# A four-layer graph network on one core: the last pass over nodes moved into the second GCN stage, with narrower PSUM slots

## The chip, the cores and the metric

The kernel runs on one core of a Trainium2 chip. The metric is the device time of one execution in microseconds; lower is better. All data are fp32. TensorE (PE in the profile, PEld for its weight loads), VectorE (DVE), ScalarE (ACT), GpSimd (POOL) and SyncE (SP) run side by side and wait for each other through semaphores. A DMA is issued from the queue of ScalarE, SyncE or GpSimd.

## What is computed

A graph of 100,000 nodes with 64 features and 50,000 edges, sorted by destination, goes through four layers. Each adds its result to x after a layer norm and a relu. The change touches the last one, a GCN of two convolutions, 64 to 32 features and back to 64:

```
def gcn_conv(x, src, dst, W, b):
    deg = segment_sum(ones_like(src), dst, n)
    dinv = where(deg > 0, rsqrt(deg), 0.0)
    norm = dinv[src] * dinv[dst]
    h = x @ W
    return segment_sum(h[src] * norm[:, None], dst, n) + b

src, dst = add_self_loops(edge_index, n)
h = relu(layernorm(x))
x = x + gcn_conv(relu(gcn_conv(h, src, dst, W1, b1)), src, dst, W2, b2)
```

The destinations are drawn as 100,000 u² with u uniform in 0 to 1: low nodes have many edges, high ones few.

## The kernel before

Nodes lie in 784 tiles of 128 (one node per partition), edges in 392 tiles of 128. Since destinations are sorted, edges and node tiles are walked together as a staircase of 74 blocks of `S` = 16 steps. A step adds one edge tile to one node tile and moves on either to the next edge tile or to the next node tile. Which it is depends on the data, so the steps of a block are loaded into registers from the small tables `g.steps` and `g.blocks` in SBUF, which `setup` makes.

The GCN consists of three stages at the end of the program, each with a block of code for every engine. An earlier stage (`sk` in the trace) has made the table t3, x @ W1 scaled by dinv, and stored x as `g.x3`.

`gcn_edges` runs twice, as first stage (t3 to t4) and as second stage (t4 to the tensor `gcn_acc` in SBUF). GpSimd gathers 128 message rows of 32 values per instruction, in 49 batches of 8 (L897 is the gather's helper line); SyncE counts the batches that arrived (L2039). VectorE makes the one-hots of a block, `hot`, in one comparison (L2095). TensorE opens the PSUM `ring` by products with the all-zero `blank` (L2071, and L2079 in mid-ring), and then adds 16 products of a one-hot with a piece of `msgs` (L2080), each to the slot of its node tile. Every fp32 product shows as two records in the trace. A slot is 128 columns wide, four times the 32 that are needed; the message columns are repeated to fill it. Two blocks are in flight: one uses the banks 0 to 3, the other 6 to 3, so they share bank 3, and its blank has to wait for the add of the block before. VectorE adds the 16 slots to the window of `gcn_acc` (L2106). In the first stage it then closes 16 tiles per block in three operations (L2121 to L2123) and ScalarE stores them; in the second stage nothing follows.

`gcn_close` is the third stage (`gf` in the trace): 49 steps of 16 tiles. VectorE scales `gcn_acc` by dinv (L2154), TensorE transposes four pieces (helper L733), ScalarE copies them to SBUF (L2179), TensorE multiplies with W2 (helper L741, N = 256), GpSimd adds the bias to the loaded x (L2203), VectorE adds the product to x (L2161), and ScalarE stores to `out` (L2191). Loads go over SyncE's queue (L2146), up to six steps ahead, stores over ScalarE's.

## Time and profile before

| | us |
|---|---|
| median of 3 runs | 6699.57 (6690.15 to 6706.76) |
| the profiled execution | 6710.78 |
| its span on the core | 6709.1 |
| busy PE / PEld | 4395.3 / 3843.5 |
| busy DVE / ACT / POOL | 4366.9 / 1838.5 / 3785.6 |

Busy shares of the whole span mix many stages. Of the 6709.1 us the three GCN stages are the last 1,268; how each is limited has to be read from its own stretch. In a timeline a row is one instruction or several merged ones ("x24"), with its start, its length, and in brackets how long its engine was idle before and what ended that. The length of a merged row reaches to the end of its last member.

### The profile page before, as it was taken

Reading aid. Unit: us, or ns where it says so; the run is one execution under the profiler, and the core shown is the slowest. Engines: PE = TensorE matmul, PEld = TensorE weight load, DVE = VectorE, ACT = ScalarE, POOL = GpSimd, SP = SyncE. Lnnn points to the kernel's source line nnn. Section 1 sums busy time; section 2 is a strip of 40 time slices with the busy share of each in tenths; the row PEclk is TensorE's granted clock in tenths of the full one; section 3 lists DMA queues with packets and bytes.
Section 4 is the critical chain, followed back from the end, with each engine's and each line's share of the span. In section 5 each row is a group of like instructions: output and inputs, shape, how many; then the busy total and the mean of one; then the engine's idle time right before and its main releaser. Section 6 shows DMA issues by size and latency. Waiting matters only on the chain. (4 is left out here: it accounts for less than half of the span.)

```text
span 6709.1 us, 96894 instructions
## 1 busy us (share of the span) xinstructions
PE 4395.3 (66%) x29117; PEld 3843.5 (57%) x29194; DVE 4366.9 (65%) x5674; ACT 1838.5 (27%) x2782; POOL 3785.6 (56%) x3348
## 2 busy tenths in 40 slices
PE   6665445771078878566565877766787856865887
PEld 3454344661067777555555865555787745755775
DVE  7898544224667778778798852224988955862458
ACT  5543112330033444333333421111453410000001
POOL 0398665773077757577763767774000047757756
PEclk9766667996589999877778988889998978988999
DMA  6398766677955558433334864544678851231109
GB/s 239 93 276 264 160 143 145 142 142 257 394 174 167 174 177 260 149 99 95 98 105 135 272 185 139 144 138 131 211 254 298 309 192 42 58 123 14 14 17 300
DMA packets 865593, 1128.43 MB, mean 168 GB/s; under 512 B 591583, under 2 KB 604276, under 8 KB 864060
## 3 DMA queue, kind: packets, MB, share of 16 engines
q1 hardware_dynamic: 409660, 807.13, 35.8%
q10 hardware_dynamic: 311296, 226.11, 11.1%
q0 software_dynamic: 144256, 90.12, 9.3%
q8 instruction: 239, 3.92, 0.2%
q14 instruction: 142, 1.16, 0.1%
HBM read 633.88 MB, written 495.44 MB: 168 GB/s over the span
## 5 line engine op out<-in xcount | busy, mean ns | idle before, releaser
L897 POOL DMA_INDIRECT gc_msgs<-t,src_rows x784 | 753.6, 961 | 1112.9 <-POOLq L148 816.2
L2080 PE MATMUL gc_ring<-gc_msgs,gc_hot 128*128 x4736 | 650.9, 296 | 239.0 <-SPq L2039 233.7
L2080 PEld LDWEIGHTS gc_ring<-gc_msgs,gc_hot 128*128 128x128 f32 x4736 | 624.2, 209 | 310.5 <-issue 303.1
L951 POOL DMA_INDIRECT acc<-de_sums,de_put x392 | 607.6, 1550 | 303.8 <-issue 149.8
L897 POOL DMA_INDIRECT edge_rows<-h,dst_rows x392 | 379.7, 969 | 231.7 <-issue 116.5
L897 POOL DMA_INDIRECT at1s_ends<-x,src_rows x392 | 409.8, 1045 | 168.7 <-issue 117.4
L897 POOL DMA_INDIRECT edge_rows<-x,dst_rows x392 | 387.7, 989 | 166.4 <-issue 117.4
L897 POOL DMA_INDIRECT re_rows<-x,src_rows x392 | 405.9, 1035 | 125.4 <-issue 125.1
L897 POOL DMA_INDIRECT at2s_ends<-h,src_rows x392 | 370.8, 946 | 142.4 <-issue 119.0
L1503 PE MATMUL re_psR<-w_rel,re_own 128*128 128x128 f32 x3136 | 396.2, 292 | 71.7 <-DVE re_own L1440 71.3
L1503 PEld LDWEIGHTS re_psR<-w_rel,re_own 128*128 128x128 f32 x3136 | 388.9, 207 | 80.5 <-issue 77.8
L2106 DVE TENSOR_TENSOR gcn_acc<-gcn_acc,gc_ring 128x512 f32 x148 | 101.7, 687 | 427.8 <-PE gc_ring L2080 427.8
L2095 DVE TENSOR_TENSOR gc_hot<-gc_fixed,steep 128x2048 f32<-128x2048 f32 x148 | 338.0, 2284 | 64.4 <-DMA gcn_acc<-t 64.4
L2179 ACT ACTIVATE gf_uT<-gf_psT 128x512 f32<-128x512 f32 x49 | 29.3, 597 | 1237.7 <-PE gf_psT L733 1237.7
L1033 DVE TENSOR_TENSOR de_sums<-de_sums,de_ring 128x64 f32 x74 | 16.4, 221 | 519.1 <-PE de_ring L1076 519.1
L1764 DVE TENSOR_TENSOR at2s_outs<-at2s_psY,at2s_own_b 128x512 f32<-128x512 f32 x196 | 135.6, 692 | 320.4 <-PE at2s_psY L741 314.1
L1076 PE MATMUL de_ring<-de_win,de_pick 128*128 x2368 | 336.3, 302 | 0.1
L1056 PE MATMUL de_ps_pick<-de_near,de_hot 128*128 x1184 | 152.8, 245 | 275.2 <-issue 233.7
L1076 PEld LDWEIGHTS de_ring<-de_win,de_pick 128*128 128x128 f32 x2368 | 321.6, 216 | 16.9 <-issue 11.0
L1301 PE MATMUL rew_ring<-rew_local,rew_hot 128*128 (+1 forms) x2368 | 283.2, 278 | 71.7 <-issue 40.4
L1301 PE MATMUL at1w_ring<-at1w_local,at1w_hot 128*128 (+1 forms) x2368 | 284.8, 279 | 62.8 <-issue 46.7
L1301 PE MATMUL at2w_ring<-at2w_local,at2w_hot 128*128 (+1 forms) x2368 | 283.5, 278 | 57.6 <-issue 45.2
(539 smaller groups left out, 11250.2 us busy)
## 6 DMA issues: line engine op xcount, KB each, us to landing
rew_win<-x SPq DMA_DIRECT2D x74, 544.0 KB
at1w_win<-g SPq DMA_DIRECT2D x74, 544.0 KB
at2w_win<-g SPq DMA_DIRECT2D x74, 544.0 KB, 4.1
de_win<-t ACTq DMA_DIRECT2D x74, 512.0 KB, 4.5
de_near<-same SPq DMA_DIRECT2D x74, 512.0 KB, 5.0
x<-rew_win SPq DMA_DIRECT2D x74, 512.0 KB
h<-at1w_win SPq DMA_DIRECT2D x74, 512.0 KB
h<-at2w_win SPq DMA_DIRECT2D x74, 512.0 KB, 2.9
```

The costliest lines, as they stand in the source:

```text
L897: nc.gpsimd.indirect_dma_start(buf[:, t * width:(t + 1) * width], None, table, bass.IndirectOffsetOnAxis(ap=rows[:, t:t + 1], axis=0)).the ...
L951: nc.gpsimd.indirect_dma_start(g.acc0[j % LANES], bass.IndirectOffsetOnAxis(ap=put[:, j:j + 1], axis=0), sums[:, j * D:(j + 1) * D], None, ...
L1033: v.tensor_tensor(here, here, low[n % 2][:, 0:D], ALU.add).then_inc(joined, 1)
L1056: done = nc.tensor.matmul(ps_pick[u % 2][:, n * P:(n + 1) * P], hot[m % 2][:, h * HALF + n, :], near[m % 3][:, bass.ds(of[n], P)], start=T ...
L1076: done = nc.tensor.matmul(ring[:, bass.ds(both[n], 2 * D)], pick[u % 2][:, n, :], win[k][:, bass.ds(both[HALF + n], 2 * D)], start=False, ...
L1301: done = nc.tensor.matmul(to[:, bass.ds(at[n], SLOT)], hot[k][:, n, :], of[:, bass.ds(at[n], SLOT)], start=False, stop=(n == S - 1), skip_ ...
L1503: last = nc.tensor.matmul(psR[s][:, t * P:(t + 1) * P], own[q][:, t * P:(t + 1) * P], each_group(g.w["rel"][:, q * D:(q + 1) * D], 2), sta ...
L1764: nc.vector.tensor_tensor(to, psY[:, :].rearrange("p (q n w) -> p q n w", n=N2, w=P), own_b[:, :, :, :].rearrange("p n u d -> p n (u d)"). ...
L2080: done = nc.tensor.matmul(ring[:, bass.ds(to[n], SLOT)], hot[k][:, n, :], each_group(msgs[:, bass.ds(of[n], MID)], SLOT // MID), start=Fal ...
L2095: nc.vector.tensor_tensor(hot[m % 2][:, :, :], each_group(fixed[:, 0:P], S), spread(g.steep[:, m * S:(m + 1) * S], P), ALU.is_equal).then_ ...
L2106: nc.vector.tensor_tensor(grouped(window, MID), grouped(window, MID), slots[(m - 1) % 2][:, :, 0:MID], ALU.add).then_inc(added, 1)
L2179: nc.scalar.activation(uT[b.slot % 2][:, :], psT[b.slot % 2][:, :], ACT.Copy).then_inc(evac, 1)
```

## The change

`gcn_close` is removed. Its work is done within the second call of `gcn_edges`, which now gets `out`: after each block's add, VectorE scales the 16 tiles that no later block changes (`scaled`), TensorE transposes them (`tip`), ScalarE copies the result (`turn`) and writes the broadcast bias into the PSUM `psO` (`fill`), TensorE accumulates the product with W2 onto it (`project`), VectorE adds `psO` to the loaded x (`finish`, three blocks later), and ScalarE stores. ScalarE issues both the loads and the stores. The groups follow the blocks, so there are 74 of 16 tiles instead of 49; neighbouring groups overlap and some tiles are written more than once with ever later sums. A store waits for the one before to land. There are two `scaled` and `scaledT`, four `x`, one `psT` and one `psO`. Where each group lies is held in four new columns of `g.blocks`, made in `setup`.

In both calls a PSUM slot is 64 columns wide instead of 128. The ring of one block takes two banks, the two blocks in flight share none, two blanks open it, and nothing is waited for in mid-ring.

```diff
@@ build
-        g.blocks = keep("blocks", [P, 6], i32)
+        g.blocks = keep("blocks", [P, 10], i32)
...
-            gcn_edges(nc, g, "gc1", g.t3, acc, g.t4)
-            gcn_edges(nc, g, "gc2", g.t4, acc, None)
-            gcn_close(nc, g, acc, out)
+            gcn_edges(nc, g, "gc1", g.t3, acc, g.t4, None)
+            gcn_edges(nc, g, "gc2", g.t4, acc, None, out)
@@ setup
+                link(v.tensor_scalar(turn[:, :], ended[:, :], float(WHOLE - S), None, ALU.min))
+                for n, unit in enumerate((1, MID, D, P)):
+                    v.tensor_scalar(g.blocks[:, 6 + n:7 + n], turn[:, :], float(unit), None, ALU.mult)
@@ gcn_edges, tiles
-        ring, fixed = r.ps("ring", [P, RING]), r.ps("fixed", [P, 512])
+        ring, fixed = r.ps("ring", [P, NARROW_RING]), r.ps("fixed", [P, 512])
+        half = NARROW_RING // 2
+            scaled, scaledT = ([r.sb(f"{n}{k}", [P, S * MID]) for k in range(2)] for n in ("scaled", "scaledT"))
+            x = [r.sb(f"x{k}", [P, S * D]) for k in range(4)]
+            psT, psO = r.ps("psT", [P, S * MID]), r.ps("psO", [P, S * D])
@@ gcn_edges, ScalarE of the second stage
+                    def load(m):
...
+                        if m > 4:
+                            act.wait_ge(done_out, 16 * (m - 4))
+                        act.dma_start(x[m % 4][:, :], part).then_inc(x_in[m % 4], 16)
+                    def turn(m):
+                        act.wait_ge(tipped, m)
...
+                        nc.scalar.activation(scaledT[m % 2][:, :], psT[:, :], ACT.Copy).then_inc(tip_copied, 1)
+                    def fill(m):
+                        if m > 1:
+                            act.wait_ge(ready, m - 1)
+                        nc.scalar.activation(grouped(psO[:, :], D), each_group(g.w["bg2"][:, :], S), ACT.Copy).then_inc(filled, 1)
+                    def store(m):
+                        act.wait_ge(ready, m)
+                        if m > 1:
+                            act.wait_ge(done_out, 16 * (m - 1))
+                        if m < BLOCKS:
+                            first = place(nc.scalar, m, 9, (WHOLE - S) * P)
+                            act.dma_start(out[bass.ds(first, S * P), :].rearrange("(j p) d -> p j d", p=P), grouped(x[m % 4][:, :], D)).then_inc(done_out, 16)
...
+                    load(1)
+                    load(2)
+                    for m in range(1, BLOCKS + 1):
+                        turn(m)
+                        fill(m)
+                        if m > 1:
+                            store(m - 1)
+                        if m + 2 <= BLOCKS:
+                            load(m + 2)
+                    store(BLOCKS)
@@ gcn_edges, TensorE
+                def tip(m):
+                    pe.wait_ge(scaled_made, m)
+                    if m > 1:
+                        pe.wait_ge(tip_copied, m - 1)
+                    transpose_pairs(nc, psT, scaled[m % 2], g.ident, S // 4).then_inc(tipped, 1)
+                def project(m):
+                    pe.wait_ge(tip_copied, m)
+                    pe.wait_ge(filled, m)
+                    times(nc, psO, scaledT[m % 2], g.w["gcn2"], S // 4, start=False).then_inc(projected, 1)
...
-                    for h in banks[k][0:3]:
-                        nc.tensor.matmul(ring[:, h * 512:(h + 1) * 512], blank[:, 0:P], blank[:, :], start=True, stop=False, skip_group_check=True)
+                        for h in range(k * half, (k + 1) * half, 512):
+                            nc.tensor.matmul(ring[:, h:h + 512], blank[:, 0:P], blank[:, :], start=True, stop=False, skip_group_check=True)
...
-                        if n == LAST_BANK:
-                            if m >= 1:
-                                pe.wait_ge(added, m)
-                            h = banks[k][3]
-                            nc.tensor.matmul(ring[:, h * 512:(h + 1) * 512], blank[:, 0:P], blank[:, :], start=True, stop=False, skip_group_check=True)
-                        done = nc.tensor.matmul(ring[:, bass.ds(to[n], SLOT)], hot[k][:, n, :],
-                                                each_group(msgs[:, bass.ds(of[n], MID)], SLOT // MID),
-                                                start=False, stop=(n == S - 1), skip_group_check=True)
+                            last = nc.tensor.matmul(ring[:, bass.ds(to[n], NARROW)], hot[k][:, n, :],
+                                                    each_group(msgs[:, bass.ds(of[n], MID)], NARROW // MID),
+                                                    start=False, stop=(n == S - 1), skip_group_check=True)
...
+                    if out is not None:
+                        if 1 <= m - 1 <= BLOCKS:
+                            tip(m - 1)
+                        if 1 <= m - 2 <= BLOCKS:
+                            project(m - 2)
@@ gcn_edges, VectorE
+                def finish(m):
+                    dve.wait_ge(x_in[m % 4], 16 * ((m - 1) // 4 + 1) if m % 4 else 16 * (m // 4))
+                    dve.wait_ge(projected, m)
+                    nc.vector.tensor_tensor(x[m % 4][:, :], x[m % 4][:, :], psO[:, :], ALU.add).then_inc(ready, 1)
...
+                    if m >= 1 and middle is None:
...
+                        dve.wait_ge(added, m)
+                        if m > 2:
+                            dve.wait_ge(tipped, m - 2)
+                        nc.vector.tensor_tensor(grouped(scaled[m % 2][:, :], MID), grouped(ended, MID), dinv, ALU.mult).then_inc(scaled_made, 1)
+                        if m > 3:
+                            finish(m - 3)
```

What stands in a row on TensorE where one block of the second stage ends and the next begins, before (an ISA row at L2080 or L2148 is the address step of the product behind it, a TENSOR_LOAD reads registers from SBUF):

```order
L2080 MATMUL gc_ring<-gc_msgs,gc_hot 128x128
L2064 TENSOR_LOAD steps
L2071 MATMUL gc_ring<-gc_blank 128x512 x3
L2072 TENSOR_LOAD blocks
L2072 ISA x2
L2080 ISA
L2080 MATMUL gc_ring<-gc_msgs,gc_hot 128x128
```

TensorE at the same place of the second stage now:

```order
L2148 MATMUL gc_ring<-gc_msgs,gc_hot 128x64
L738 MATMUL gc_psT<-ident,gc_scaled 128x128 x4
L746 MATMUL gc_psO<-w_gcn,gc_scaledT 128x256 x4
L2137 TENSOR_LOAD steps
L2144 MATMUL gc_ring<-gc_blank 128x512 x2
L2145 TENSOR_LOAD blocks
L2145 ISA x2
L2148 ISA
L2148 MATMUL gc_ring<-gc_msgs,gc_hot 128x64
```

Four transposes and four products (of 256 columns) have come between the last product of a ring and the register load of the next block, and two blanks of three are left at the start.

On ScalarE, one step in the middle of the last pass before:

```order
L2194 ISA
L2178 REGISTER_ALU
L2179 ACTIVATE gf_uT<-gf_psT 128x512
L2191 ISA
L2191 DMA out_x<-gf_x 128x16x64
```

ScalarE over one block in the middle of the second stage now, where it had nothing before:

```order
L2089 ACTIVATE gc_scaledT<-gc_psT 128x512
L2094 ACTIVATE gc_psO<-b_bg 128x1024
L2056 TENSOR_LOAD blocks
L2102 ISA
L2102 DMA out_x<-gc_x 128x16x64
L2056 TENSOR_LOAD blocks
L2083 REGISTER_ALU
L2083 DMA gc_x<-x 128x1024
```

A second activation, the load of x and two register loads have joined the copy and the store.

On VectorE, one block of the second stage before:

```order
L2095 TENSOR_TENSOR gc_hot<-gc_fixed,steep 128x2048
L2101 TENSOR_LOAD blocks
L2106 ISA
L2106 TENSOR_TENSOR gcn_acc<-gcn_acc,gc_ring 128x512
L2095 TENSOR_TENSOR gc_hot<-gc_fixed,steep 128x2048
```

VectorE over one block of the second stage now:

```order
L2174 TENSOR_TENSOR gc_hot<-gc_fixed,steep 128x2048
L2056 TENSOR_LOAD blocks
L2185 ISA
L2185 TENSOR_TENSOR gcn_acc<-gcn_acc,gc_ring 128x512
L2206 TENSOR_LOAD blocks
L2216 ISA
L2216 TENSOR_TENSOR gc_scaled<-gcn_acc,dinv 128x512
L2168 TENSOR_TENSOR gc_x<-gc_x,gc_psO 128x1024
L2174 TENSOR_TENSOR gc_hot<-gc_fixed,steep 128x2048
```

The scaling and the last add, of a group three blocks older, have moved between the add of a block and the one-hots of the next but one.

## Rows read from the trace of the kernel before

**Rows 1.** Windows: stretch, us, busy PE, PEld, DVE, ACT, POOL; granted clock, DMA share, GB/s.
```profile
5441.00:6001.00 560.00, 384.48 (x2626) 329.40 (x2664) 367.19 (x373) 0.00 (x0) 382.87 (x392) 0.88 0.24 71
6001.00:6537.00 536.00, 385.22 (x2627) 330.66 (x2664) 214.77 (x152) 0.00 (x0) 370.73 (x392) 0.88 0.15 37
6537.00:6709.10 172.10, 127.64 (x588) 95.27 (x588) 141.64 (x98) 29.26 (x49) 116.91 (x49) 0.96 1.07 298
```

**Rows 2.** Waits of the second stage (who waited for whom: us, times, longest).
```profile
...
PE gc_ring L2080 <- SPq L2039: 118.0, 20, 31.0
...
```

**Rows 3.** Timeline, second stage, GpSimd: start us, us, engine line op [idle before].
```profile
6249.63 0.95 POOL L897 DMA_INDIRECT gc_msgs<-t,src_rows  x1 [0.31 <-issue]
```

**Rows 4.** Timeline, second stage, VectorE: adds of blocks 12, 21, 30, 35 and 74.
```profile
6167.42 0.69 DVE L2106 TENSOR_TENSOR gcn_acc<-gcn_acc,gc_ring 128x512 f32 x1 [4.27 <-PE gc_ring L2080]
...
6239.26 0.69 DVE L2106 TENSOR_TENSOR gcn_acc<-gcn_acc,gc_ring 128x512 f32 x1 [7.14 <-PE gc_ring L2080]
...
6300.30 0.69 DVE L2106 TENSOR_TENSOR gcn_acc<-gcn_acc,gc_ring 128x512 f32 x1 [9.22 <-PE gc_ring L2080]
...
6329.03 0.69 DVE L2106 TENSOR_TENSOR gcn_acc<-gcn_acc,gc_ring 128x512 f32 x1 [6.02 <-PE gc_ring L2080]
...
6535.21 0.69 DVE L2106 TENSOR_TENSOR gcn_acc<-gcn_acc,gc_ring 128x512 f32 x1 [4.57 <-PE gc_ring L2080]
```

**Rows 5.** Timeline, second stage, weight loads: one late block.
```profile
6387.01 0.34 PEld L2071 LDWEIGHTS gc_ring<-gc_blank 128*128 128x128 bf16 x3 [0.59 <-issue]
6387.81 2.75 PEld L2080 LDWEIGHTS gc_ring<-gc_msgs,gc_hot 128*128 128x128 f32 x24 [0.46 <-issue]
6390.49 0.10 PEld L2079 LDWEIGHTS gc_ring<-gc_blank 128*128 128x128 bf16 x1
...
6392.23 0.34 PEld L2071 LDWEIGHTS gc_ring<-gc_blank 128*128 128x128 bf16 x3 [0.56 <-issue]
```

**Rows 6.** Timeline, second stage, weight loads after a ring at a lower clock.
```profile
6237.85 1.08 PEld L2080 LDWEIGHTS gc_ring<-gc_msgs,gc_hot 128*128 128x128 f32 x8
6238.85 0.42 PEld L2071 LDWEIGHTS gc_ring<-gc_blank 128*128 128x128 bf16 x3
```

**Rows 7.** Timeline, stage before the GCN, TensorE: products 64 and 128 columns wide.
```profile
5296.04 2.00 PE L741 MATMUL sk_psO<-w_gcn,sk_hT 128*128 128x64 f32 x16 [1.82 <-ACT sk_hT L1951]
5297.87 2.00 PE L741 MATMUL sk_psB<-w_skip_b,sk_g2T 128*128 128x128 f32 x16
```

**Rows 8.** Timeline, last pass, TensorE: the products, then the transposes of one tile.
```profile
6644.81 1.99 PE L741 MATMUL gf_psH<-w_gcn,gf_uT 128*128 128x256 f32 x8 [0.69 <-ACT gf_uT L2179]
6646.64 0.60 PE L733 MATMUL gf_psT<-ident,gf_u 128*128 128x128 f32 x4
```

**Rows 9.** Timeline, first stage, weight loads: a late block opens.
```profile
5859.49 0.34 PEld L2071 LDWEIGHTS gc_ring<-gc_blank 128*128 128x128 bf16 x3 [1.12 <-issue]
```

**Rows 10.** Timeline, first stage, VectorE: adds of blocks 35 and 74, one block between.
```profile
5774.68 0.69 DVE L2106 TENSOR_TENSOR gcn_acc<-gcn_acc,gc_ring 128x512 f32 x1 [5.66 <-PE gc_ring L2080]
...
5858.71 0.69 DVE L2106 TENSOR_TENSOR gcn_acc<-gcn_acc,gc_ring 128x512 f32 x1 [0.41 <-PE gc_ring L2080]
...
5861.61 2.28 DVE L2095 TENSOR_TENSOR gc_hot<-gc_fixed,steep 128x2048 f32<-128x2048 f32 x1
...
5995.21 0.69 DVE L2106 TENSOR_TENSOR gcn_acc<-gcn_acc,gc_ring 128x512 f32 x1 [2.57 <-PE gc_ring L2080]
```

**Rows 11.** Instructions of three tiles: ns min/median/max, first and last start us.
```profile
L2154 DVE TENSOR_TENSOR gf_u<-gcn_acc,dinv x49: 685/1905/2480, 6536.9 to 6696.8; 128x512 f32 x42, 128x512 f32<-128x512 f32 x7
...
L2161 DVE TENSOR_TENSOR gf_x<-gf_x,gf_psH x49: 1207/1222/1223, 6543.6 to 6702.3; 128x1024 f32<-128x1024 f32 x49
...
L1266 ACT ACTIVATE rew_ring<-rew_blank x74: 807/810/1437, 2403.0 to 2741.3; 128x780 f32<-128x780 f32 x72, 128x1536 f32<-128x1536 f32 x2
```

**Rows 12.** Tile out_x in the last pass: issue to landing of its stores.
```profile
DMA to landing us min/median/max: 3.8/6.1/7.0
```

**Rows 13.** Timeline, last pass, VectorE: its last add.
```profile
6702.27 1.22 DVE L2161 TENSOR_TENSOR gf_x<-gf_x,gf_psH 128x1024 f32<-128x1024 f32 x1 [2.24 <-PE gf_psH L741]
```

More of the change, by code:

```diff
@@ L2003, in _, with gcn_edges @@
                 pipeline(dve, order=[(3, close), (2, variance), (1, add)], slots=DEEP)
-def gcn_edges(nc, g, name, nodes, acc, middle):
+def gcn_edges(nc, g, name, nodes, acc, middle, out):
     W = B * MID
-    LAST_BANK = 3 * 512 // SLOT
     with Room(nc, g, name) as r:
@@ L2039, in _, with place @@
                     sp.sem_inc(arrived, 1)
-            if middle is not None:
-                @block.scalar
-                def _(act):
+            def place(eng, m, column, last):
+                at = eng.alloc_register(f"{name}_{column}_{m}")
+                eng.load(at, g.blocks[m:m + 1, column:column + 1])
+                return eng.snap(at, donate=True, min_val=0, max_val=last)
+            @block.scalar
+            def _(act):
+                if middle is not None:
                     to = middle.rearrange("(p t) d -> p (t d)", t=PITCH)
@@ L2208 @@
+                if middle is None:
+                    for m in range(BLOCKS - 2, BLOCKS + 1):
+                        finish(m)
 NAMES = ["x", "src", "dst", "edge_attr_32", "edge_type_8", "edge_weight1", "L0_gnn_b", "L1_gnn_weight",
```

147 lines of the change are left out of this document (54 added, 93 removed).

## The prediction, made before the changed kernel was run

> **What bounds the kernel now.** I read the windows of the three last stages first: 560, 536 and 172.1 us, 1,268 of the 6,709.1 us span [rows 1]. The change touches these three alone, apart from six small instructions at the start. In the first two GpSimd gathers messages and TensorE sums them, 74 blocks of 16 steps each; in the third every node tile is closed.
>
> The waits come next. In the second stage TensorE waited 118.0 us, 20 times, for a gathered batch [rows 2]. GpSimd issues one gather each 1.25 us (0.95 of work, 0.31 between) [rows 3], so 392 gathers take 490 us and set the early blocks, where many edges go to few nodes. The adds on VectorE date the blocks [rows 4]: block 35 ends at 6329.03 and block 74 at 6535.21. From there 39 blocks take 206.2 us, 5.29 each, and nothing waits for a gather. This is TensorE's own pace; one late block shows of what it consists [rows 5]. Three blank products open the ring and a register load follows, 0.80 us; 32 weight loads with a fourth blank among them last until about 6391.68, 3.87 us; then the weight queue is idle 0.56 us while 32 registers are loaded. The sum is 5.23. VectorE is busy for 214.77 us of 536 [rows 1], so it has room.
>
> The third stage moves 298 GB/s, and VectorE is busy for 141.64 of 172.1 us [rows 1]. One tile group costs it 1.22 us for the last add, and a scaling whose median is 1.91 although its shortest is 0.69 [rows 11], while GpSimd adds the bias beside it.
>
> **The change, part by part.**
>
> *Third stage gone.* It removes 172.1 us, and 5.6 us of these come back: from the end of the last add, 6703.49 [rows 13], to the end of the span the last stores are issued and land. That is in the tail below.
>
> *Narrower ring matmuls.* The moving operand falls from 128 to 64 columns. In the stage before the GCN, 16 instructions of 64 columns and 16 of 128 both take 2.00 us [rows 7], with weights of the same size. I therefore book nothing. (The Trainium skill, "TensorE: Matmul & The Clock Gate", section "Back-to-back issue gap", gives a gap that falls with the columns, 134 cycles for 128 and about 60 up to 64; by that the ring would take about half. The same page, section "LDWEIGHTS (loading the stationary operand)", ties a weight load to the weight's own columns, which do not change.) The row decides; what half would give is a rival.
>
> *Blanks.* Four become two, and they cover separate halves, so the wait for the add in mid-ring goes. The mid-ring blank moved the loads behind it by 0.1, the products by 0.2; one opening blank fewer gives 0.11 (0.34 for three). I take 0.32 us a block.
>
> *First stage.* 39 blocks lie between 5774.68 and 5995.21, 5.65 us each [rows 10]. TensorE needs 5.79 from opening to opening there, with 1.12 us of register loading [rows 9]. VectorE's floor is close: from the add at 5858.71 to the end of the one-hot at 5863.89 is 5.18 us [rows 10]. Thus 5.65 becomes 5.33, above the floor, and 39 × 0.32 = 12 us go. Bounds: 5.21 gives 17; if TensorE's load wait just grows, 0.
>
> *Second stage, TensorE.* Each block now also has four transposes and eight product records of 256 columns. From products to transposes is 1.83 us; four transposes take 0.60 with the last one's latency, 0.45 without (0.27 of latency, as four spacings of 0.11) [rows 8]. A late block is then: two blanks 0.43, ring 3.70 (3.87 without the mid blank), transposes 0.45, products 1.83, 6.41 in all. To it comes what register loads do not hide. After a ring at full clock they cost 0.56 to 1.12 [rows 5, 9]. After a ring that ran slower than it was issued they cost nothing: the blanks start at 6238.85, before the last of eight loads from 6237.85 is over [rows 6]. The products are such work: 0.23 each, where ring records are issued at 0.115, so the sequencer gains some 0.9 us on the array. I take 0.2 and get 6.6 us. The bounds are 6.4 and 7.8 (1.12 in full, and a ring that starts 0.26 later after its blanks).
>
> *What hides the rest.* VectorE per block: one-hot 2.28, add 0.69, scaling 0.69 (the shortest of rows 11, since GpSimd no longer works beside it), last add 1.22, 4.9 us in all, under 6.6. ScalarE: copy to SBUF, bias into PSUM (128x1024, which from 0.81 us for 780 columns [rows 11] is about 1.06), two DMA issues and two register loads, under 4 us. There is one psO, so last add, bias fill, products and last add again form a ring: 1.22 + 1.06 + 1.99 and some waits, 4.5 us, also under 6.6. If either cover fails it becomes the pace. Loads move from SyncE's queue to ScalarE's, where each stands behind a store; SyncE keeps only the arrivals. A block adds up to 1 MB of traffic in 6.6 us, half the rate at which the third stage runs now. Two x loads beside the first read of acc delay the first batch by some 3 us, which later gathers do not inherit.
>
> *Where the stage ends.* With slower blocks the last batch that holds TensorE up lies earlier. I take the latest of (add time + blocks left × period) over blocks that were set by a gather [rows 4]: block 21, 6239.26 + 53 × 6.6 = 6589.1; block 30, 6300.30 + 44 × 6.6 = 6590.7; block 35, 6329.03 + 39 × 6.6 = 6586.4. The last ring's add starts at 6590.7. Gathers may slow by a few per cent beside the new traffic, up to 8 us here.
>
> *Tail.* After this add the products of tile group 71 finish at +2.5 and its last add at +3.7. Groups 72, 73 and 74 pass the ring of 4.5 us one after another: +17.2. The last store waits until the one before has landed (3.8 to 7.0 us [rows 12]), some 2 us more, and 5.6 us follow as now. Together 25 us, to 6615.7.
>
> *Sum.* 6615.7 − 6709.1 = −93.4; first stage −12; start +1. That is −104 us. The profiled execution was 6710.78 us and would become 6606; the median of the runs, 6699.57, lies 11 us lower, and on it the forecast is 6596 us.
>
> **The rivals.**
>
> A. *Half the columns, half the ring.* TensorE would need about 4.8 us a block and VectorE's 4.9 plus its waits, about 5.3, would set the pace. Then 6329.03 + 39 × 5.3 = 6535.7, +25; with 14 us in the first stage the saving is 161, time 6538. For it: a product's own work does fall with its columns. Against: the equal 2.00 us [rows 7]. (The rule of the Trainium skill named above is this rival.) Chance 0.07.
>
> B. *The register loads stay bare.* If a wait for a semaphore in front of transposes or products keeps the sequencer from getting ahead, the period is about 7.5: 6239.26 + 53 × 7.5 = 6636.8, +25 = 6661.8, or −47; −11 for first stage and start. Time 6641. For it: 0.56 to 1.12 us in every late block now. Against: the blanks of rows 6, which also stand behind a wait. Chance 0.13.
>
> C. *The stores become the chain: slower than before.* Each store waits until the one before has landed, with a register load of 0.47 and an issue of 0.38 in between, so the period is at least landing + 0.9. The turning point: for block 12, 6167.42 + 62 × p + 25 − 11 = 6709.1 gives p = 8.5, a landing of 7.6 us. At 8.1 us, p = 9.0: 6167.42 + 558 + 25 = 6750.4, or +41 and −11, time 6730. For it: a median of 6.1 us [rows 12], now with the loads on the same queue and gathers beside. Against: these were measured at 298 GB/s [rows 1], and even the longest, 7.0, is short of 7.6. Chance 0.04.
>
> **How the numbers follow.** The forecast has 0.74, A 0.07, B 0.13, C 0.04; 0.02 are left for something around no change. The forecast's own range is −9 for a period of 6.4, −5 for the first stage at VectorE's floor, −5 for a shorter tail and −7 if these stages gain from a better clock: 6570; and up to +12 for no gain in the first stage, +8 for slower gathers. B lies above, at 6641 and +9 for its own spread. The range 6570 to 6650 leaves out A, C and a little of the others. A change of 0.3%, 20 us, is about what can be told from none; faster has 0.93, same 0.03, slower 0.04.
>
> **What would show it.** In the profile after: 64-wide ring loads still 0.11 us apart (A: less). Late blocks of the second stage 6.6 us apart with TensorE hardly idle (B: idle before the blanks). The third stage gone, and about 25 us between the last ring add and the end. First stage 12 us shorter, its late blocks at 5.3. VectorE's scaling at 0.69. Waits on ScalarE for stores that do not reach TensorE; a TensorE wait for psO or its bias, or stores that take over 7 us to land, would prove me wrong, as would gathers well over 1.25 us apart.

## The result, and the profile after

The changed kernel took **6732.26 us** (median, 6725.98 to 6736.3); the kernel before took 6705.2 us beside it. The ratio is **1.0043, with a 95% interval of 1.0033 to 1.0053**: slower by 27 us in the medians (29 us by the ratio), where 104 us of gain were forecast, and outside the range. The profiled span is 6734.4 us, against 6604.7 in the forecast's own sum (6615.7 − 12 + 1).

The adds on VectorE date the blocks again. First, the timeline of VectorE after the change (start, length, line, operation, idle before): blocks 35 and 74 of the first stage, then 35 and 74 of the second.

```profile
5784.12 0.69 DVE L2185 TENSOR_TENSOR gcn_acc<-gcn_acc,gc_ring 128x512 f32 x1 [2.39 <-PE gc_ring L2148]
...
6079.48 0.69 DVE L2185 TENSOR_TENSOR gcn_acc<-gcn_acc,gc_ring 128x512 f32 x1 [4.60 <-PE gc_ring L2148]
...
6436.15 0.69 DVE L2185 TENSOR_TENSOR gcn_acc<-gcn_acc,gc_ring 128x512 f32 x1 [1.62 <-PE gc_ring L2148]
...
6709.17 0.69 DVE L2185 TENSOR_TENSOR gcn_acc<-gcn_acc,gc_ring 128x512 f32 x1 [3.76 <-PE gc_ring L2148]
```

From these four starts the whole difference can be placed:

| stretch | forecast, us | measured, us | too little by |
| --- | --- | --- | --- |
| to the last add of the first stage | 5984.2 (5995.21 − 12 + 1) | 6079.48 | 95.3 |
| from there to the last ring add of the second | 595.5 (6590.7 − 5995.2) | 629.7 | 34.2 |
| from there to the end of the span | 25.0 | 25.2 | 0.2 |

So three quarters of the miss lie in the *first* stage, where the only edits were the narrower ring (columns, slots, places of its waits) and two blanks fewer. Its 74 blocks took 599.5 us from first add to last (5479.97 to 6079.48); before it was 513.0 (5482.20 to 5995.21). So 86.5 us were lost and the 12 us of gain did not come; it began 3.2 us earlier than booked. There 39 late blocks took 295.4 us, 7.57 each (5.65 in [rows 10]). The windows say why (columns as in [rows 1]; the first whole stretch is the one of its first line):

```profile
5441.00:6001.00 560.00, 486.40 (x2165) 456.38 (x2164) 314.33 (x316) 0.00 (x0) 372.59 (x390) 0.50 0.23 64
...
6000.00:6050.00 50.00, 50.00 (x225) 47.44 (x226) 31.79 (x32) 0.00 (x0) 0.00 (x0) 0.50 0.10 38
6100.00:6150.00 50.00, 17.85 (x79) 16.59 (x80) 9.45 (x7) 0.00 (x0) 37.92 (x40) 0.50 0.52 190
6150.00:6200.00 50.00, 35.94 (x175) 31.84 (x175) 17.98 (x15) 6.39 (x8) 37.97 (x40) 0.67 0.38 87
...
6250.00:6300.00 50.00, 45.07 (x321) 39.00 (x321) 32.54 (x27) 10.93 (x14) 38.12 (x40) 0.99 0.61 148
...
6320.00:6380.00 60.00, 56.11 (x313) 50.99 (x314) 29.20 (x25) 9.75 (x12) 45.66 (x48) 0.76 0.56 133
...
6450.00:6650.00 200.00, 186.37 (x1307) 157.07 (x1305) 137.11 (x116) 46.12 (x58) 100.97 (x104) 1.00 0.66 160
```

**The granted clock of TensorE was 0.50, its lower level of 1.2 GHz, through the whole first stage** (0.88 before). It was busy for 486.40 of 560 us there, more than before, and from 6000 to 6050 without any gap in the profile: a busy engine at half clock. In the second stage, where transposes and products stand behind each ring, the clock rises from 0.67 to 0.99, falls once more from 6320 to 6380 (0.76), and is 1.00 in the late blocks from 6450 to 6650. Weight loads of one late block of the first stage:

```profile
5988.04 0.36 PEld L2144 LDWEIGHTS gc_ring<-gc_blank 128*128 128x128 bf16 x2
5988.68 7.16 PEld L2148 LDWEIGHTS gc_ring<-gc_msgs,gc_hot 128*128 128x128 f32 x32 [0.28 <-issue]
5995.61 0.36 PEld L2144 LDWEIGHTS gc_ring<-gc_blank 128*128 128x128 bf16 x2
```

A load takes 0.22 us of the queue (7.16 / 32), twice the 0.115 of [rows 5]. No idle time stands in front of the blanks: at this pace the sequencer is ahead, as in [rows 6].

In the second stage two of the late blocks looked like this (same view):

```profile
6501.31 0.13 PEld L2144 LDWEIGHTS gc_ring<-gc_blank 128*128 128x128 bf16 x2 [0.76 <-issue]
6502.21 3.65 PEld L2148 LDWEIGHTS gc_ring<-gc_msgs,gc_hot 128*128 128x128 f32 x32 [0.77 <-issue]
6505.73 0.48 PEld L738 LDWEIGHTS gc_psT<-ident,gc_scaled 128*128 128x128 f32 x4
6506.17 1.60 PEld L746 LDWEIGHTS gc_psO<-w_gcn,gc_scaledT 128*128 128x128 f32 x8
6508.17 0.13 PEld L2144 LDWEIGHTS gc_ring<-gc_blank 128*128 128x128 bf16 x2 [0.40 <-issue]
```

Ring loads are 0.114 us apart with 64 columns as with 128 [rows 5]; transposes and products follow without a gap. But in front of the blanks the queue was idle for 0.76 and 0.40 us (0.64 on average over the ten blocks from 6500 to 6570), where the forecast had 0.2. In the late stretch a block took 7.01 us, where 6.6 was booked.

The late blocks are only about half of what the second stage lost. Its last 39 blocks took 273.0 us (257.4 booked, 15.6 too little); the other 18.6 of the 34.2 us were lost before block 35. Blocks 23, 25 and 27 took 9.9 to 10.3 us each, with 7.2 to 7.3 between, though TensorE waited for no gather: after 1.3 to 1.5 us of idle time before the blanks, part of the ring ran at the lower clock. This is block 27:

```profile
6372.09 0.13 PEld L2144 LDWEIGHTS gc_ring<-gc_blank 128*128 128x128 bf16 x2 [1.38 <-issue]
6373.05 5.99 PEld L2148 LDWEIGHTS gc_ring<-gc_msgs,gc_hot 128*128 128x128 f32 x32 [0.83 <-issue]
```

So the lower clock cost about 9 us here too, three blocks of some 3 us each.

The waits of the second stage and tail (who waited for whom: us, times, longest) show that nothing else took over:

```profile
ACT gc_psO L2094 <- DVE gc_x L2168: 190.3, 73, 4.1
...
PE gc_ring L2148 <- SPq L2052: 68.8, 13, 33.8
DVE gc_x L2168 <- PE gc_psO L746: 57.0, 65, 5.1
...
ACT gc_scaledT L2089 <- DMA out_x<-gc_x: 24.2, 7, 3.8
```

TensorE's waits for gathers fell from 118.0 us [rows 2] to 68.8, and ScalarE waited for a store only seven times. The 190.3 us are time in which ScalarE waited to fill psO; TensorE waited for that fill 6.6 us in all.

### The profile page after: what moved, and what is told of

Its sections match the earlier page's. It is cut to its first block and busy times, and to the rows that moved or that the text cites. A ratio compares the mean times of both kernels' runs of the same rounds, so it can differ in the third digit from the quotient of the medians.

```text
span 6734.4 us, 97436 instructions
## 1 busy us (share of the span) xinstructions
PE 4598.7 (68%) x29198; PEld 4078.2 (61%) x29198; DVE 4366.9 (65%) x5729; ACT 1930.0 (29%) x2881; POOL 3673.1 (55%) x3299
## 5 line engine op out<-in xcount | busy, mean ns | idle before, releaser
L2148 PEld LDWEIGHTS gc_ring<-gc_msgs,gc_hot 128*128 128x128 f32 x4736 | 824.9, 272 | 222.7 <-issue 216.5
L2148 PE MATMUL gc_ring<-gc_msgs,gc_hot 128*128 x4736 | 827.2, 357 | 153.7 <-SPq L2052 142.4
L2089 ACT ACTIVATE gc_scaledT<-gc_psT 128x512 f32<-128x512 f32 x74 | 44.2, 597 | 983.8 <-PE gc_psT L738 958.2
```

The source lines that it names most:

```text
L2089: nc.scalar.activation(scaledT[m % 2][:, :], psT[:, :], ACT.Copy).then_inc(tip_copied, 1)
L2148: last = nc.tensor.matmul(ring[:, bass.ds(to[n], NARROW)], hot[k][:, n, :], each_group(msgs[:, bass.ds(of[n], MID)], NARROW // MID), start ...
```

## The experiments

Two theories had to be told apart for the first stage: (1) products of 64 columns leave TensorE at its lower clock; (2) the clock fell for another reason: the two blanks fewer, or the changed slots and waits. For the second stage the question was what the idle time before the blanks depends on. Late periods below are means of the last 30 blocks of a stage. The kernel before had medians of 6696.0 to 6704.6 us beside these runs.

**b_cols64: the kernel before, only the product narrower.** Slots stay 128 wide, four blanks stay, in both stages.

```diff
-done = nc.tensor.matmul(ring[:, bass.ds(to[n], SLOT)], hot[k][:, n, :],
-                        each_group(msgs[:, bass.ds(of[n], MID)], SLOT // MID),
+done = nc.tensor.matmul(ring[:, bass.ds(to[n], 64)], hot[k][:, n, :],
+                        each_group(msgs[:, bass.ds(of[n], MID)], 64 // MID),
```

> The kernel before with one edit: a ring product writes 64 columns instead of 128, into slots that stay 128 wide in the seven-bank ring. Blanks, waits, layout and the last pass are those of before. Theory (the number of moving columns alone keeps TensorE at its lower clock): granted clock 0.50 in most of both GCN stages, late blocks at about 8.4 us (7.57 as after, and 0.86 for two more blanks at that clock), each stage about 150 us longer, time near 7000 us. Rival (the new ring layout, with its two blanks and without the wait in mid-ring, is what lowers it): clock and time as before, 6705 us within 20. Rival of my prediction (columns are work): both stages shorter than before.

Measured: 6747.02 us, ratio 1.0073 (1.005 to 1.0096). The direction is that of theory 1, the size is not. Two windows of its first stage:

```profile
5600.00:5650.00 50.00, 48.10 (x207) 43.84 (x211) 28.61 (x30) 0.00 (x0) 38.01 (x39) 0.50 0.16 40
...
5950.00:5980.00 30.00, 24.70 (x184) 20.68 (x187) 26.06 (x28) 0.00 (x0) 0.00 (x0) 1.00 0.12 45
```

The early blocks run at 0.50 and take 8.3 us; later the clock goes up and down and ends at 1.00, where blocks take 5.1 to 5.9 us. From first add to last the stage took 538.6 us, against 513.0 before. The second stage, which the theory had at half clock too, took 540.9 us from last add to last add, against 540.0 before: its early blocks ran at 0.50 to 0.84, and its late ones at 1.00 with the old period of 5.31. The narrow product alone lowers the clock, but with four blanks a block it does not hold it down to the end.

**b_cols96: the same with 96 columns.** The edit is the one above with 96 in place of 64.

> As the run with 64 columns, with 96. The theory does not say on which side 96 falls. If the clock is granted again, late blocks are at 5.3 (second stage) and 5.65 us (first), and time is that of before; if not, they are above 8 us as with 64 columns. If the cost of a product grew with its columns at a given clock, 96 would lie evenly between 64 and 128; I expect no such thing, since 64 columns take 0.22 us a record after, and 128 columns took 0.22 before wherever the granted clock was low.

Measured: 6697.58 us, ratio 1.0 (0.9989 to 1.0011). The first stage in one window:

```profile
5441.00:6001.00 560.00, 383.68 (x2626) 334.37 (x2664) 368.74 (x375) 0.00 (x0) 388.81 (x394) 0.87 0.24 71
```

Beside 384.48 us busy and 0.88 in [rows 1] nothing moved: neither clock nor time. So 96 columns and 128 cost the same; at the upper level the columns do not count, as [rows 7] had it.

**b_narrow_ring: the changed kernel's ring in both stages, with the last pass left apart as before.** Slots and products of 64 columns and two blanks; no transposes or products in the second stage.

```diff
-            gcn_edges(nc, g, "gc2", g.t4, acc, None, out)
+            gcn_edges(nc, g, "gc2", g.t4, acc, None, None)
+            gcn_close(nc, g, acc, out)
...
```

> The changed kernel's ring (64-wide slots, two blanks, no wait in mid-ring) in both stages, with the separate last pass of before kept. Theory: granted clock 0.50 in both stages, 7.57 us a block, first stage +84 us, second stage 6239.26 + 53 x 7.57 = 6640.5 for its last block, +105 us, time near 6895 us. It says too that it is the products and transposes of the merged pass that raise the clock in the second stage of the changed kernel. Rival (the clock is low in the first stage for another reason, such as what ran before): the second stage has a high clock here too, about 5.0 us a block, time near 6770 us.

Measured: 6891.57 us, ratio 1.0282 (1.026 to 1.0304). A window of each stage:

```profile
5850.00:5900.00 50.00, 49.34 (x223) 47.45 (x226) 31.80 (x33) 0.00 (x0) 37.88 (x40) 0.50 0.18 45
6400.00:6450.00 50.00, 49.13 (x221) 47.44 (x225) 20.22 (x14) 0.00 (x0) 37.81 (x41) 0.50 0.09 14
```

Both stages stay at 0.50, and late blocks take 7.57 us in both. This shows two things. The ring half of the edit costs some 195 us when it stands alone. And the merged pass, which brings 256-column products and transposes into each block, is what lifts the clock in the changed kernel's second stage; whether the products or the transposes do it the runs don't separate.

**a_wide_first: the changed kernel, with the first stage's ring as before** (128 columns, 128-wide slots, three blanks and one in mid-ring; the second stage keeps the narrow ring). The table of register values becomes 64 columns wide, to hold both kinds of place.

```diff
-        g.steps = keep("steps", [P, 3 * S], i32)
+        g.steps = keep("steps", [P, 4 * S], i32)
...
+        if middle is not None:
+            ring = r.ps("ring", [P, RING])
+            slots = [grouped(ring[:, 0:S * SLOT], SLOT), grouped(ring[:, RING - S * SLOT:RING], SLOT)[:, ::-1, :]]
...
+                        wide = NARROW if middle is None else SLOT
-                            last = nc.tensor.matmul(ring[:, bass.ds(to[n], NARROW)], hot[k][:, n, :],
+                            last = nc.tensor.matmul(ring[:, bass.ds(to[n], wide)], hot[k][:, n, :],
...
```

> The changed kernel with the first stage's ring as before (128 columns, four blanks, wait in mid-ring); the second stage stays as changed. Theory: first stage back at about 5.65 us a late block and 84 us shorter than in the changed kernel, second stage as in the changed kernel at 7.08 us a late block; time 6732 - 84 = 6648 us, 0.85% faster than before. Rival (the first stage is slow for another reason than its products): time stays near 6732 us.

Measured: **6606.79 us, ratio 0.9866 (0.9846 to 0.9885)**. The first stage is back at its old clock:

```profile
5441.00:6001.00 560.00, 384.54 (x2626) 329.99 (x2663) 367.64 (x373) 0.00 (x0) 382.38 (x391) 0.88 0.23 69
```

From first add to last it takes 515.0 us (5468.55 to 5983.57), 84.5 less than in the changed kernel, and near the 513.0 of before. But the spans differ by 131.2 us. Of the rest 11.4 lie ahead of the stage (it began anywhere between 5468.6 and 5487.3 in the profiled runs, with the same code ahead of it), and 35.8 in the second stage: 593.9 from last add to last ring add against 629.7, with a late period of 6.53 instead of 7.01, though no line of it was touched. The kernels that follow go after each of the two: a_blanks6 after the clock of the first stage, those from a_pad to b_space after the period of the second.

**a_blanks6: the changed kernel, with six blanks a block in the first stage instead of two.** The added products multiply zeros and add zeros.

```diff
+                            for again in range(2 if middle is not None else 0):
+                                nc.tensor.matmul(ring[:, h:h + 512], blank[:, 0:P], blank[:, :], start=False, stop=False, skip_group_check=True)
```

> The changed kernel, with six blanks per block instead of two in the first stage: each bank gets two more products of zeros, 512 columns each, that add zero. They cost 4 x 0.21 us at the upper clock and 4 x 0.43 at the lower. Theory (how many columns stream through the array per time decides the granted clock, whatever they hold): the first stage is granted the upper clock for most of its late blocks, which take about 6.2 us instead of 7.57, and the whole kernel some 40 us less than the changed one. Rival (products of zeros do not count): the clock stays 0.50, blocks take 7.57 + 1.7 = 9.3 us and the kernel over 80 us more than the changed one.

Measured: 6640.05 us, ratio 0.9901 (0.9885 to 0.9918). That is 92 us less than the changed kernel, for more work, where some 40 were expected. Windows of the first stage:

```profile
5700.00:5750.00 50.00, 43.56 (x298) 36.68 (x302) 37.68 (x40) 0.00 (x0) 38.12 (x39) 0.90 0.20 51
5850.00:5900.00 50.00, 42.68 (x316) 36.45 (x320) 41.83 (x43) 0.00 (x0) 38.42 (x39) 0.97 0.22 60
```

The products are still 64 columns wide, in the same slots, behind the same waits; only zeros were added, and the clock is 0.90 to 0.97 and the late period 5.77 us. This rules the slots and the waits out as what holds the clock down. The second stage kept its 7.01. What remains is how much TensorE is given: narrow products with four blanks had the clock at 0.68 and with two at 0.50. Two blanks with products of 128 columns were not run, so what the missing blanks do by themselves is not shown.

**a_pad: the changed kernel with a register table of 64 columns instead of 48**, nothing else.

```diff
-        g.steps = keep("steps", [P, 3 * S], i32)
+        g.steps = keep("steps", [P, 4 * S], i32)
```

> The changed kernel with one edit: the table of steps in SBUF is 64 columns wide instead of 48, the last 16 unused; each row of it then begins at another address. In the run with the wide first stage, whose second stage has the same instructions as the changed kernel's, late blocks took 6.52 us instead of 7.01, and the idle time before the blanks fell from 0.62 to 0.09 us a block; that kernel had the wider table too. If the place of the tables decides how long a register load takes, late blocks of the second stage take about 6.5 us here and the kernel about 20 us less than the changed one, with the first stage still at 0.50. If not (the load is shorter for what the first stage did, or where the code lies), nothing changes.

Measured: 6696.2 us, ratio 0.9994 (0.9984 to 1.0003), 36 us less than the changed kernel. The first stage is unchanged (7.57); the second stage's late period is 6.51. So sixteen unused words account for the second gain. They make a row of the table 256 bytes long and also move every tensor behind it by 64 bytes; this run does not say which of the two matters. (The kernel before ran 6 us faster beside this run than beside the changed kernel; ratio against ratio the gain is 0.5%, 33 us.)

**a_space_behind and a_space_around: which tensors the 64 bytes have to move.** Both are the changed kernel with unused columns beside the table of blocks, which is allocated behind the register table: the first only behind it, the second before and behind.

```diff
         g.blocks = keep("blocks", [P, 10], i32)
+        keep("spacer", [P, 16])
```

> The changed kernel with 64 unused bytes per partition behind the table of blocks. Both register tables stay where they are (steps at byte 27584, blocks at 27776); all that is allocated later (the weights w_gcn2, gcn_acc, messages, one-hots, x) moves up by 64 bytes, to where it lies in the run with the wider table (gcn_acc at 29440, a multiple of 256; in the changed kernel 29376). If the place of the large tensors is what made late blocks of the second stage 6.51 us instead of 7.01, they take 6.5 us here and the kernel takes about 6696 us. If the place of the table of blocks does, they take 7.0 us and the kernel 6732 us.

> The other way round: 64 unused bytes ahead of the table of blocks and 64 behind it. The table of blocks lies where it lay in the run with the wider table (27840), the large tensors 128 bytes above their place in the changed kernel (gcn_acc at 29504, which leaves 64 over a multiple of 256). If the table of blocks decides, late blocks take 6.5 us; if the large tensors do and want more than a multiple of 64, 7.0 us.

Measured: 6703.03 us, ratio 0.9998 (0.9984 to 1.0012), late period 6.50, and 6728.06 us, ratio 1.0045 (1.0028 to 1.0062), late period 7.02. My theory that the register table itself mattered fell with the first: neither table's row changed in it, and the gain was there. A move of everything behind by 64 bytes helps, one by 128 does not.

**a_space_stage and a_space_scaled: which of them.** The spacer now stands inside the second stage alone, before all its own tensors, or behind messages, one-hots and blank, so that only the scaled tiles, their transposed copies and the x rows move.

```diff
+            r.sb("spacer", [P, 16])
             scaled, scaledT = ([r.sb(f"{n}{k}", [P, S * MID]) for k in range(2)] for n in ("scaled", "scaledT"))
             x = [r.sb(f"x{k}", [P, S * D]) for k in range(4)]
```

> The changed kernel with 64 bytes of spare SBUF in front of the second stage's own tensors: messages, one-hots, blank, scaled tiles and x rows move by 64 bytes, while the accumulator, the GCN weight and everything earlier stay. Theory 1: it is the place of the stage's own tensors (weights of the ring, written one-hots, x rows) that makes the idle time before the blank products 0.62 us a block. Then late blocks of the second stage come 6.50 us apart instead of 7.01, as with the spacer behind the block table, and the time is about 6700 us. Theory 2: it is the place of the accumulator or the GCN weight; then the period stays at 7.01 and the time at 6732 us.

> The changed kernel with 64 bytes of spare SBUF behind the second stage's messages, one-hots and blank: only the scaled tiles and the x rows move. If the stage's own tensors matter, this divides them. Theory 1a (messages and one-hots, which the ring reads): nothing changes, period 7.01, 6732 us. Theory 1b (scaled tiles or x rows, the operands of the merged pass, which the kernel before does not have): period 6.50, 6700 us. If the accumulator or the GCN weight is the cause: nothing changes, 6732 us.

Measured: 6694.5 us, ratio 0.9987 (0.9975 to 1.0), and 6696.86 us, ratio 0.9984 (0.9974 to 0.9993); both have a late period of 6.51. The second settles it: moving the merged pass's own operands by 64 bytes is enough. In the late blocks (groups of weight loads from 6500 to 6570: count, busy us, mean ns, idle before) the blanks show it, first the changed kernel, then a_space_scaled:

```profile
L2144 PEld LDWEIGHTS gc_ring<-gc_blank 128*128 128x128 bf16 x20 | 1.3, 95 | 6.4 <-issue 6.4
```

```profile
L2145 PEld LDWEIGHTS gc_ring<-gc_blank 128*128 128x128 bf16 x20 | 1.7, 96 | 2.0 <-issue 1.1
```

6.4 us idle in ten blocks became 2.0. The profile puts this idle time down to "issue", but the same trace shows the instruction that stands there, the load of TensorE's 32 registers for the next block (ns: shortest, median, longest; from 6420 to 6670). First the changed kernel, then a_space_scaled:

```profile
L2137 PEldq TENSOR_LOAD <-steps x36: 2677/3079/3485, 6421.2 to 6666.6; - x36
```

```profile
L2138 PEldq TENSOR_LOAD <-steps x39: 2369/2532/2787, 6417.9 to 6665.2; - x39
```

The load became 0.55 us shorter and the period 0.50. This holds in all runs: in late blocks its median is 3.07 to 3.09 us in the three kernels with a period of about 7.0, 2.51 to 2.55 in the six with 6.5, and 2.18 to 2.19 in the second stages without the merged pass. So the place of the merged pass's operands acts on TensorE through the time of its register load, although neither the registers' table nor the load had changed.

The x rows' transfers changed too. The first line of each pair is ScalarE's time for issuing the loads of x (same three numbers), the second the time to landing; changed kernel, then a_space_scaled, both from 6420 to 6670:

```profile
L2083 ACTq DMA_DIRECT2D gc_x<-x x36: 428/972/2160, 6419.9 to 6665.3; - x36
...
DMA to landing us min/median/max: 4.6/5.5/6.8
```

```profile
L2084 ACTq DMA_DIRECT2D gc_x<-x x38: 339/534/2561, 6424.0 to 6664.5; - x38
...
DMA to landing us min/median/max: 3.7/4.5/5.8
```

The medians of the issue fall into the same two groups as the periods: 937 to 1043 ns in the three kernels with about 7.0 us a block (the changed one, a_space_around, a_blanks6), 527 to 563 in the six with 6.5 (stretches of 130 to 250 us behind 6400). The slow issue of x loads and the slow register load thus go together. Whether one delays the other, or both suffer from a third thing, no run shows; nor is it shown whether the x rows alone, without the scaled tiles, would do.

**b_space: the same 64-byte step in the kernel before**, with 96 bytes behind its block table, which put the accumulator at the same address as in a_space_behind.

```diff
         g.blocks = keep("blocks", [P, 6], i32)
+        keep("spacer", [P, 24])
```

> The kernel before with 96 unused bytes behind its table of blocks, so that gcn_acc lies at 29440 as in the run with the wider table, instead of 29344; the tables stay. If the place of the large tensors shortens register loads there too, late blocks of the second stage, now 5.3 us with 0.6 us idle before the blanks, and those of the first, 5.65, get shorter and the kernel takes 10 to 40 us less than before. Otherwise it takes the same.

Measured: 6698.24 us, ratio 0.9998 (0.9988 to 1.0007), late periods 5.65 and 5.30 (before: 5.69 and 5.30). The kernel before gains nothing. That fits: its two `gcn_edges` stages have no x rows and no scaled tiles.

**a_best: a_wide_first with the table's columns put in another order**, so that the first stage loads its 32 registers at once and not in two loads of 16.

```diff
...
-                            nc.tensor.load(regs[0:S], g.steps[m:m + 1, 0:S])
-                            nc.tensor.load(regs[S:2 * S], g.steps[m:m + 1, 3 * S:4 * S])
+                            nc.tensor.load(regs[S:2 * S] + regs[0:S], g.steps[m:m + 1, 0:2 * S])
```

> The kernel with the wide first stage, its three groups of step columns in an order in which each stage takes its 32 registers in one load. The first stage had two loads there, and late blocks of 5.78 us against 5.69 before. Expected: 5.7 us or a little less in the first stage, the second as in that run (6.52), and 3 to 5 us less in all, about 6603 us, 1.4% under the kernel before. If the place of a row's first column matters for the load, the second stage, which now starts 64 bytes into the row, shows another idle time before its blanks.

Measured: **6607.64 us, ratio 0.9862 (0.9846 to 0.9879)**. The first stage's late period falls from 5.78 to 5.66, but the time is that of a_wide_first within their spread. The second stage's period stays at 6.51, so the place of the row's first column made no difference. Both kernels beat the one before by 1.3 to 1.4%. The last adds of the two stages in a_best:

```profile
5983.45 0.69 DVE L2204 TENSOR_TENSOR gcn_acc<-gcn_acc,gc_ring 128x512 f32 x1 [2.55 <-PE gc_ring L2167]
```

```profile
6577.08 0.69 DVE L2204 TENSOR_TENSOR gcn_acc<-gcn_acc,gc_ring 128x512 f32 x1 [3.09 <-PE gc_ring L2167]
```

Eight of the kernels in one table. "Columns" are those of a ring product in the first stage, "blanks" those of one block there, "clock" is the granted clock from 5441 to 6001:

| kernel | columns, blanks | clock | late period, first / second stage | time, us |
| --- | --- | --- | --- | --- |
| before | 128, 4 | 0.88 | 5.69 / 5.30 | 6705.2 |
| b_cols96 | 96, 4 | 0.87 | 5.70 / 5.30 | 6697.58 |
| b_cols64 | 64, 4 | 0.68 | changing / 5.31 | 6747.02 |
| b_narrow_ring | 64, 2 | 0.50 | 7.57 / 7.57 | 6891.57 |
| after | 64, 2 | 0.50 | 7.57 / 7.01 | 6732.26 |
| a_blanks6 | 64, 6 | 0.82 | 5.77 / 7.01 | 6640.05 |
| a_space_scaled | 64, 2 | 0.50 | 7.57 / 6.51 | 6696.86 |
| a_best | 128, 4 | 0.89 | 5.66 / 6.51 | 6607.64 |

## Why the prediction was wrong, point by point

**Narrower ring matmuls: the step that failed.** The prediction took from [rows 7] that the columns cost no time, and booked nothing. At the upper clock that holds: a ring record takes 0.114 us with 64 columns as with 128 (24 loads in 2.75 us, b_cols64 and [rows 5]), and the time with 96 is that of before. What it left out is that the clock itself depends on what TensorE is given. [rows 7] show a short piece, two rows of 16 records at the upper clock, and cannot show what 600 us of such products do. Fewer columns took no time from the ring at a held clock, but the ring as a whole, with its two blanks fewer, stayed at 1.2 GHz, where a record takes 0.22 us. a_wide_first gives the price of both together: 84.5 us in the first stage. Of this the narrower product alone, with four blanks, makes some 26 (b_cols64: 538.6 against 513.0 us).

**Blanks and first stage.** "12 us go" came out as +84 (5995.21 to 6079.48). The working could hold only at an unchanged clock. The removed blanks, 512 columns each, were not only a cost: with them back and two more in a_blanks6 the stage ran at 5.77. The bounds given for the first stage (0 to 17 us of gain) allowed for no loss. The clock stood in the forecast only as a gain, 7 us at the lower end of the range, although [rows 1] showed it at 0.88 and [rows 6] showed what a slower ring looks like. That it could be lost was the rival that was missing. Whether two blanks fewer give 12 us at a held upper clock was not tried: no run had two blanks and that clock.

**Second stage, TensorE.** The order of the work was right, but the sum came close partly by luck. Means from the timeline of the weight loads, over 27 late blocks of the changed kernel and 30 of a_space_scaled, with what was booked:

| | booked, us | changed kernel | a_space_scaled |
| --- | --- | --- | --- |
| blanks, until the ring starts | 0.43 | 0.84 | 0.83 |
| ring, until the transposes start | 3.70 | 3.51 | 3.51 |
| transposes | 0.45 | 0.45 | 0.45 |
| products | 1.83 | 1.60 | 1.60 |
| idle before the next blanks | 0.2 | 0.62 | 0.13 |
| period | 6.6 | 7.01 | 6.52 |

The blanks were booked 0.41 too low: a register load stands behind them too, and [rows 5] show 0.80 us there with three blanks. Ring and products were booked 0.42 too high together, which hid it. What was left is the last term, the register load that the products do not hide: 0.2 booked, 0.62 measured. The load takes 3.08 us there, against 2.18 in the kernel before, and 2.53 once the operands lie elsewhere. The period was inside the bounds of 6.4 to 7.8, and near rival B's 7.5 without being it, for B's reason (a semaphore wait that holds the sequencer) is not the cause: with unchanged waits and other addresses the period is 6.51. With them nothing of the 34.2 us is left: a_space_scaled needs 592.1 us for the stretch booked at 595.5. In the slow place the stretch depends on the clock too: a_space_around, with the same late period but blocks 23 to 34 at about 7.0 us each, needed 617.7 us, 12 less than the changed kernel.

**The low clock at the start of the second stage** cost nothing lasting. a_space_scaled and a_best begin their second stages at 0.50 too (a_best from 6035 to 6060, though its first stage had 0.89) and need 592.1 us (6679.06 − 6086.93) and 593.6 us from last add to last add. The gathers set the pace there. The booked value was 595.5. The dips after the gathers have stopped holding TensorE up, from 6320 to 6380 in the changed kernel, did cost, as told above.

**What hides the rest** held. VectorE's scaling and ScalarE's fill of the bias (groups from 6500 to 6570, mean ns behind the comma) came at 0.694 and 1.028 us, for 0.69 and 1.06 booked:

```profile
L2094 ACT ACTIVATE gc_psO<-b_bg 128x1024 f32<-128x1024 f32 x10 | 10.3, 1028 | 24.6 <-DVE gc_x L2168 24.6
...
L2216 DVE TENSOR_TENSOR gc_scaled<-gcn_acc,dinv 128x512 f32 x10 | 6.9, 694 | 3.4 <-DVE gcn_acc L2185 3.4
```

**The tail** held in its sum: from the last ring add at 6709.17 to the end 25.2 us, for 25. Its last add on VectorE, below, is over after 19.9 us (17.2 booked), and 5.3 follow (7.6 booked), so two errors of 2.5 us cancel:

```profile
6727.84 1.22 DVE L2168 TENSOR_TENSOR gc_x<-gc_x,gc_psO 128x1024 f32<-128x1024 f32 x1 [5.07 <-PE gc_psO L746]
```

**The rivals.** A (half the ring) is refuted: 32 loads in 3.65 us. And in b_cols64 at the clock of 1.00, 24 loads from 5968.55 took 2.75 us, as with 128 columns in [rows 5]. The Trainium skill, "TensorE: Matmul & The Clock Gate", section "Back-to-back issue gap", gives, for products by themselves, a gap that falls with the columns. In this ring, where each product brings a weight load of its own, the rows differ from it. B is refuted as a mechanism. C (stores as the chain) is refuted too, although the kernel did get slower, as C had it: ScalarE waited for stores 24.2 us in all, seven times, and TensorE waited for ScalarE's fill only 6.6 us. Getting slower for another reason is no support for C.

Of the forecast's terms, then, the tail stands, the second stage stands once the operands lie elsewhere (with errors inside it that cancel), and the first stage falls. a_best, with the merged pass, the old first ring and that other place, needs 593.6 us in the second stage (595.5 booked) and 23.0 behind it (6577.08 to 6600.1; 25 booked). Its median of 6607.64 lies near the 6596 forecast, but for a kernel other than the one forecast. The value of merging the pass was read rightly in sum; that the narrower slots and fewer blanks come free was not.

## What to carry to other kernels

Before making TensorE's work smaller, look at the granted clock of the stage. Where narrow and wide products take equal time, as here with a weight load for each, narrowing saves nothing and can leave the whole stage at half clock; keep the old width where it fits (here in the first stage) or pay for some zero products. Give the clock a term and a rival of its own in every sum that changes what TensorE streams. When a queue waits for nothing that the profile names, look at how long its register loads take, and try the same kernel with its tensors moved by 64 bytes: here that was worth 0.5% (in one stage of one kernel, and nothing in the kernel before).

## What the runs showed that I had not expected

- More work was faster: four added zero products a block made the kernel 92 us shorter (6732.26 to 6640.05), with the first stage's clock at 0.82 instead of 0.50.
- A busy engine can sit at the lower clock: 50.00 of 50 us busy at 0.50, and 486.40 of 560 us in the whole stage. (The ends of products are modelled in the profile, so this busy time is not a measure of work in the array.) What the engine did in the rows is all that can be said: 64-column products with two blanks stayed low, with four they changed level within the stage, with six they were at 0.90 and above from 5700 on in the windows shown, and with 96 or 128 columns and four blanks they ran as before. The Trainium skill, "TensorE: Matmul & The Clock Gate", section "Part 1: The HAM clock gate", has the gate set by how busy TensorE has been. By the busy time of the profile that would give the upper clock from 6000 to 6050; the trace shows 0.50.
- Fewer blanks and narrower products cost 195 us when the pass stands alone (b_narrow_ring), in both stages. With the pass merged they cost the 84.5 of the first stage and some 9 in the second: one half of the change hid half of what the other lost.
- A shift of 64 bytes of the merged pass's operands is worth 0.5 us a late block and 25 to 38 us in all (6694.5 to 6703.03 us in the four kernels with nothing but unused bytes added, 6728.06 and 6732.26 in the slow place). It shows as idle time of TensorE, of which the profile says only "issue", and as a register load of 2.5 instead of 3.1 us; a shift of 128 bytes is worth nothing. In the slow place the load of x rows takes ScalarE 0.97 us to issue instead of 0.53.
